# New places for some steps in the hand-set order of every engine, in a fused attention and mixture kernel

## What is computed

```python
x = x + attention(cond(x, side, side, w1, u1, cond_512), Wq, Wk, Wv, Wo, q_scale, k_scale)
x = x + ffn(cond(x, side, side, w2, u2, cond_512), gate_w, mask_up_w, gate_proj_w, up_proj_w, down_proj_w)
```

## Time and profile before

| what | value |
|---|---|
| median of 3 runs | 415.3 us |
| the profiled execution | 415.59 us |
| its span on the core | 413.8 us |
| PE busy | 367.6 us (89%) |
| DVE busy | 326.0 us (79%) |
| ACT busy | 275.6 us (67%) |
| POOL busy | 218.7 us (53%) |
| chain that ended last | PE 66%, DVE 19%, ACT 11%, issue 3% |

### The profile page before, as it was taken

One profiled execution on the slowest core, in us unless ns is written; L12 is line 12 of the kernel. 1 busy time (PEld: TensorE's weight loads), 2 busy tenths in 40 slices (PEclk: granted clock), 3 DMA queues, 4 the chain that ended last, 5 costly groups with the idle time before them and its releaser, 6 DMA issues.

```text
span 413.8 us, 6407 instructions
## 1 busy us (share of the span) xinstructions
PE 367.6 (89%) x1952; PEld 295.0 (71%) x1952; DVE 326.0 (79%) x759; ACT 275.6 (67%) x673; POOL 218.7 (53%) x230
## 2 busy tenths in 40 slices
PE   0098869899999799898999997999899999999996
PEld 0097656688878667687787776687687878788884
DVE  8999789988988997599999889476567777665543
ACT  5547789798789497796978879784274434453321
POOL 7260614278524868134693121563269756888832
PEclk9999999999999999999999999999999999999999
DMA  6825300112100304001031000110065433365121
GB/s 207 308 76 197 104 0 3 49 57 99 52 0 2 103 0 154 1 2 51 2 101 40 1 2 0 38 48 32 2 186 160 140 115 97 96 216 166 53 76 51
DMA packets 14209, 31.92 MB, mean 77 GB/s; under 512 B 1872, under 2 KB 4432, under 8 KB 14176
## 3 DMA queue, kind: packets, MB, share of 16 engines
q1 hardware_dynamic: 13888, 31.38, 23.2%
q10 hardware_dynamic: 288, 0.14, 0.1%
HBM read 30.43 MB, written 1.08 MB: 76 GB/s over the span
## 4 chain that ended last, share of the span: by engine, by line
PE 66%; DVE 19%; ACT 11%; issue 3%; DVEq 0%; ACTq 0%
PE ov L1223 7%; PE sc L1201 7%; PE tr L1152 5%; PE proj L1140 4%; PE acc L1126 3%; PE acc L1128 3%; PE acc L1127 3%; PE proj L1144 3%; PE proj L1141 3%; PE acc L1317 2%; PE acc L1318 2%; PE tr L1127 2%; PE acc L1321 2%; PE tr L1126 2%; PE tr L1128 2%
## 5 line engine op out<-in xcount | busy, mean ns | idle before, releaser
L598 POOL TENSOR_TENSOR WL<-stage,WH 128x256 fp32r<-128x256 f32 x142 | 125.6, 913 | 75.6 <-ACT WH L664 75.6
L612 POOL TENSOR_TENSOR PR<-PR,RI 128x512 f32<-128x512 f32 x48 | 53.7, 1134 | 80.7 <-DVE RI L1072 80.7
L1140 PE MATMUL proj<-WH,RH 128*128 128x512 f32 x96 | 42.5, 442 | 32.0 <-DVE RL L923 19.9
L625 ACT ACTIVATE PR<-PR,MX 128x128 f32<-128x128 f32 (+1 forms) x128 | 56.6, 455 | 0.0
L1201 PEld LDWEIGHTS sc<-kT,QT 128*128 128x128 f32 x256 | 41.0, 191 | 15.8 <-issue 12.8
L1223 PE MATMUL ov<-PTS,V 128*128 128x512 f32 x96 | 46.6, 594 | 1.1 <-DVE OL L1084 1.1
L1201 PE MATMUL sc<-kT,QT 128*128 128x128 f32 (+1 forms) x256 | 47.2, 327 | 0.0
L1140 PEld LDWEIGHTS proj<-WH,RH 128*128 128x128 f32 x96 | 18.4, 192 | 38.6 <-issue 36.3
L1062 DVE CUSTOM_DVE_ANT_0 PR<-sc,const,RQ 128x128 f32<-128x128 f32 (+1 forms) x128 | 45.5, 411 | 0.1
L824 ACT CAST OH<-PR 128x512 fp32r<-128x512 f32 x22 | 13.6, 620 | 41.7 <-DVE PR L1108 41.7
L618 POOL TENSOR_TENSOR OL<-PR,OH 128x512 fp32r<-128x512 f32 x22 | 28.9, 1315 | 22.3 <-ACT OH L824 20.8
(11 more groups left out here) (166 smaller groups left out, 948.4 us busy)
## 6 DMA issues: line engine op xcount, KB each, us to landing
stage<-in_ffn SPq DMA_DIRECT2D x22, 384.0 KB, 3.3
stage<-in_wq SPq DMA_DIRECT2D x8, 512.0 KB, 3.3
stage<-in_wo SPq DMA_DIRECT2D x8, 512.0 KB, 3.3
SBC<-group_scalars SPq DMA_DIRECT2D x8, 256.0 KB, 3.6
PR<-in_tables SPq DMA_DIRECT2D x4, 352.0 KB, 7.4
fT<-in_fT SPq DMA_DIRECT2D x4, 256.0 KB, 4.0
xT<-in_xT SPq DMA_DIRECT2D x4, 256.0 KB, 4.5
stage<-in_wk SPq DMA_DIRECT2D x2, 512.0 KB, 4.9
```

The source lines that it names most:

```text
L598: i = pool.tensor_tensor(lo[:, c:c + 256], src[:, c:c + 256], hi[:, c:c + 256].bitcast(F32), ALU.subtract)
L612: pool.tensor_tensor(pr, pr, RI[:, m % 4, hs[0]:hs[0] + nh].rearrange("p (h o) -> p h o", o=1).broadcast_to([P, nh, 512 // nh]), ALU.mult) ...
L625: return nc.scalar.activation(o, i, ACT.Exp, **k)
L1140: mm(proj[:], rh[ch], wh[ch], start=ch == 0, stop=False, skip_group_check=True)
```

## The change

It moves steps and changes none. At the start, TensorE runs both late table products R6 and R7 ahead of the first query projection; ScalarE casts Q0 behind its copy of K1(0,0); VectorE makes the key weights' low part WL and the next batch's E ahead of RL. In the tiles, VectorE's pattern has "rest" and a "bg" ahead of "D1"; onehot goes from tile 2 to 3; V1's split from 17 to 15; Q7's split from 23 to 25; K3(1,2) and K3(1,3) from 19 to 20; V(1,1) from 21 to 22. All lines below the first insertion carry a number that is one higher in the changed kernel.

```diff
@@ ORDERS
-    "DVE": [("kv", 0), ("kv", 0), ("bg", 0), ("kv", 0), ("bg", 0), ("A", 0), ("D1", 4),
-            ("kv", 0), ("bg", 0), ("F", 6), ("N", 0), ("S", 2), ("rest", 0), ("kv", 0),
+    "DVE": [("kv", 0), ("kv", 0), ("bg", 0), ("kv", 0), ("bg", 0), ("A", 0), ("rest", 0),
+            ("bg", 0), ("D1", 4), ("kv", 0), ("F", 6), ("N", 0), ("S", 2), ("kv", 0),
@@ START
-           ("R", 2), ("R", 3), ("R", 4), ("R", 5), ("K3", 0, 0), ("K3", 0, 1)],
+           ("R", 2), ("R", 3), ("R", 4), ("R", 5), ("K3", 0, 0), ("K3", 0, 1), ("R", 6),
+           ("R", 7)],
@@ START, ACT
-            ("split", "K", 0), ("wkv", 1, 0, 7), ("small",), ("wkv", 1, 1, 1), ("split", "Q", 0), ("K1", 0, 0), ("K1", 0, 1),
+            ("split", "K", 0), ("wkv", 1, 0, 7), ("small",), ("wkv", 1, 1, 1), ("K1", 0, 0), ("split", "Q", 0), ("K1", 0, 1),
@@ START, DVE
-    "DVE": [("wkv", 1, 0, 0), ("wkv", 1, 0, 2), ("wkv", 1, 0, 3), ("wkv", 1, 0, 4), ("wkv", 1, 0, 5), ("wkv", 1, 0, 6), ("wkv", 1, 0, 8),
-            ("wkv", 1, 1, 0), ("split", "K", 0), ("wkv", 1, 1, 2), ("wkv", 1, 1, 3), ("wkv", 1, 1, 4), ("K1", 0, 0), ("K1", 0, 1),
+    "DVE": [("wkv", 1, 0, 0), ("wkv", 1, 0, 2), ("wkv", 1, 0, 3), ("wkv", 1, 0, 4), ("wkv", 1, 0, 5), ("wkv", 1, 0, 6), ("split", "K", 0),
+            ("wkv", 1, 1, 0), ("wkv", 1, 0, 8), ("wkv", 1, 1, 2), ("wkv", 1, 1, 3), ("wkv", 1, 1, 4), ("K1", 0, 0), ("K1", 0, 1),
@@ make_plan
-                  (2, ("onehot",)), (15, ("zeros",)),
-                  (10, ("split", "K", 1)), (17, ("split", "V", 1))):
+                  (3, ("onehot",)), (15, ("zeros",)),
+                  (10, ("split", "K", 1)), (15, ("split", "V", 1))):
...
-    for n, back in enumerate([-2, -2, -2, -1, -3, -2, -2, -3]):
+    for n, back in enumerate([-2, -2, -2, -1, -3, -2, -2, -1]):
...
-    for half, places in (((0, 1), [2, 4, 4, 5, 6]), ((1, 0), [15, 15, 15, 17, 18]), ((1, 1), [17, 18, 18, 19, 19])):
+    for half, places in (((0, 1), [2, 4, 4, 5, 6]), ((1, 0), [15, 15, 15, 17, 18]), ((1, 1), [17, 18, 18, 20, 20])):
...
-    for p, places in ((0, [3, 5, 6, 6]), (1, [21, 21, 23, 24])):
+    for p, places in ((0, [3, 5, 6, 6]), (1, [21, 22, 23, 24])):
```

## The result

The changed kernel takes 416.92 us (median of 5 executions, 416.34 to 417.44), the kernel before 415.3 (5 executions, 415.06 to 415.86). The ratio is 1.0035 with a 95% interval of 1.0024 to 1.0046: 1.0 to 1.9 us slower. The profiled execution of the changed kernel took 417.44, the highest of its five, with a span of 415.6, so its trace holds some more than the median difference (1.8 in the spans, 415.6 against 413.8).

The account below looks back on a forecast made before the run. Chain on VectorE until 42.6 us, then mostly TensorE, waiting for ScalarE's copies. Terms 0.3 + 0.2 + 0.6 + 0.2 = 1.3, given as 1.2 above the 415.3 median: 416.5 us, range 413.6 to 417.8.

Parts of the forecast that it names:

- Edit 1: Start, reordered on TensorE, ScalarE and VectorE: 0.3 us slower, bounds -0.9 and +0.5.
- A(0) comes out at -0.9 or -0.4 + 1.2: Start: VectorE's kept saving of 0.4 to 0.9, plus R7's 1.2, puts A(0) 0.3 to 0.8 us later.
- Edit 2: Onehot moved from tile 2 to 3, ahead of the sum for A(3): 0.2 us slower, bounds 0 and 0.7.
- its first part: Onehot at its new place: 0.41 us on VectorE up to its second instruction.
- Edit 3: V1's split at tile 15, O3's cast behind E(10), delaying K1(1,2)'s copy: 0.6 us slower, bounds 0 and 0.97.
- Edit 4: K3(1,2), K3(1,3), V(1,1) and Q7's split moved later: 0.2 us slower, bounds -1.4 and +0.8.
- Rival A: Start and tiles 19 on: relief of the VectorE-GpSimd lock reaches TensorE, 1.9 us less, 413.4; chance 0.26.
- B: Whole kernel: ScalarE has hidden slack at V1's split, the rest cancels, no difference, 415.3; chance 0.22.
- C: RL behind GWL, onehot at upper bound, V1's split, A(22)'s 0.8 kept: 2.6 us more, 417.9; chance 0.10.

Follow-up runs that it names:

- the three lists alone: Kernel before with only the start's reorderings on VectorE, ScalarE and TensorE: 416.04 us, ratio 1.0012.
- VectorE's list alone: Kernel before with only VectorE's start reordered, WL and E ahead of RL: 414.69 us, ratio 0.9984.
- ScalarE's list alone: Kernel before with only ScalarE's cast of Q0 behind the copy of K1(0,0): 414.98 us, ratio 0.9992.
- GpSimd held back: Changed kernel with one added wait, so GpSimd's gate piece GWL starts behind RL: 415.78 us, ratio 1.0008 to the kernel before.
- VectorE's list and the last edits: Kernel before with VectorE's new start, K3 to tile 20, V(1,1) to 22, Q7's split to 25, wkv(2,2,1) a tile later: 414.48 us, ratio 0.9976.

## Why the prediction was right, and where it was right by luck

Forecast 416.5, measured 416.9, on the side it was expected.

**Edit 1, +0.3:** the three lists alone give +0.5 (0.1 to 0.9). Its steps, one by one: first matmul 0.8 to 1.3 later, measured 1.46 with 0.24 of DMA, so 1.22, near the end where RL pays for GWL; scans at 1.2, yes; VectorE idle before the sum of K1(0,1), yes, 2.04; TensorE idle between A(0) and B(0), yes, 0.68. R7 was priced at 1.2 at A(0), of which ScalarE makes up 0.2 to 0.3 by A(1): 1.19 and 1.05 at these two copies where R7 was moved alone, so this held but for 0.1. One step was wrong. "A(0) comes out at -0.9 or -0.4 + 1.2" takes VectorE as what sets K3. The trace of the kernel without R7's move agrees (K3 0.72 sooner), but the profiled changed kernel has K3 0.57 later, since there TensorE was the later one. I had let TensorE's own way from the first matmul to K3 out of the sum: it was 1.08 ahead of VectorE before, and a first matmul 1.22 later uses up more than that. This is the step that failed. The expectation for VectorE's list alone had TensorE's wait in it and missed too (+0.5 against -0.7), by leaving out what VectorE gains.

**Edit 2, +0.2:** the two instructions take 0.18 and 0.25 at the new place (0.38 and 0.65 before) and ScalarE's wait grew from 0.32 to 0.36. 0.03 in the trace. The term was mis-sized in its first part: the cast holds VectorE for 0.22 there and not for 0.41; the second instruction holds it for 0.17 and E gives back 0.34, as worked out. Neither onehot's move nor the new place of "rest" and "bg" in VectorE's pattern was run alone.

**Edit 3, +0.6:** 0.44 to 0.47 in the traces, 0.7 (0.4 to 1.1) in the time. The step (a cast of 1.07 in place of an idle 0.32) is what the trace shows; the copy of K1(1,2) makes up 0.44 of it and not 0.32. The wait before A(17) was to be 1.4 and is 0.93, because TensorE already waits 0.20 for ScalarE's copy of QT a little ahead of it.

**Edit 4, +0.2:** A(21) and A(22) came out as worked out: -1.94 against -1.9 forecast, +0.81 against +0.8, each taken from the 1.88 at A(17). The wait at D(21,1) went, as forecast. What was mis-sized is what that gives back: the row at 264.01 shows -0.2 for the edit in all, so 1.0 is taken back behind tile 22, and not 0.6. Alone it measured 0.

**The sum.** The runs alone give 0.5 for the start, 0.7 for edit 3 and 0 for edit 4: 1.2 with onehot's 0.03, the forecast's own size, and the changed kernel 1.5 (1.0 to 1.9). That they add holds within the intervals. That the sum fits is in part luck. In the trace of the changed kernel the start is 1.1 above its term and the other three together some 0.7 below theirs (0.03, 0.44 and -0.2 against 0.2, 0.6 and 0.2), and these errors cancel.

Rival A fell. A part of what it counts on is there without R7: VectorE's list alone gives -0.7, but by the wait of 0.68 that it fills, since RL then pays for GWL in a scan's place. Freeing one scan brought K1(0,2) 0.32 sooner with ScalarE's list alone, and nothing behind VectorE's list. Its condition, ScalarE at V(1,1) before TensorE, is met in the kernel with wkv(2,2,1) later, and that is 0.5 faster. B would have been the result without R7's move. C's 0.8 of A(22) was not kept.

## What to carry to other kernels

Where two engines arrive at one place, write down both arrivals before costing a move: one that delays the early engine is free up to its wait, and what goes beyond the wait is paid for. A filler between a projection and its transposes (R7 here) costs nothing while it covers the wait for the copy; ahead of the projection nearly all of it is paid for (1.03 of 1.2). When one step leaves a tile, look at what stands ahead of its copy on the engine that drains the bank: moving those three activations turned a null result into a gain.

## What the runs showed of the hardware

**The lock falls on whichever two-input instruction stands beside GpSimd's piece.** RL took 1.22 beside the gate piece and 0.68 to 0.69 where that piece was held back; a scan 1.69 against 1.20; a sum of squares 0.68 in either case. The Trainium skill (SBUF — State Buffer, "Who interferes with whom") says that the later one to issue is fully blocked and that a reduction never is, and these traces agree with both.

**TensorE starts slowly, for a time that differs from trace to trace.** With nothing before, its first matmuls of 512 columns follow each other by 0.43 us (1.2 GHz by the columns), later ones by 0.23 (near 2.4 GHz), while the page's granted clock is 1.00 in both stretches. The way from the first matmul to R1 holds the same 20 matmuls in every kernel here (14 of them up to the second projection) and took these times:

| kernel | first matmul | to the second projection | to R1 |
|---|---|---|---|
| before | 19.89 | 4.81 | 6.51 |
| changed | 21.35 | 4.82 | 6.86 |
| changed, R7 back | 21.23 | 4.16 | 5.62 |
| GpSimd held back | 20.58 | 4.17 | 5.62 |
| K3 and V(1,1) moved alone | 19.89 | 4.63 | 6.14 |
| the same, wkv(2,2,1) later | 19.88 | 4.82 | 6.42 |
| R7 moved alone | 19.88 | 4.61 | 6.12 |
| VectorE's list alone | 21.11 | 4.82 | 6.50 |
| VectorE's list and the last edits | 21.10 | 4.40 | 5.90 |

The same work takes up to 1.24 more in one execution than in another. The order is not the reason: the changed kernel and the one with R7 back have the same order on every engine up to K3 and took 6.86 and 5.62, and the kernel before and the two with only tiles 19 and later moved took 6.51, 6.14 and 6.42. In the latter three TensorE's wait at K3 (1.08, 1.47 and 1.19) hides the difference: K1(0,2) stands at 44.67 to 44.70 in all of them. In the changed kernel it lies on the path, and the profiled execution has the longest one. With K3 at 32.89, as in the kernel with R7 back, and 11.9 to 12.1 from there, K1(0,2) would stand at 44.8 to 45.0: 0.1 to 0.3 later than before, which is the forecast's term. The trace has it at 46.08. What sets the length of the slow stretch stays open, and so does some 0.5 of the 1.5 us between the changed kernel and the same with R7 back, of which R7's place explains 1.0 to 1.1.

**A second place differs from trace to trace.** Near 312 us, behind the last product of a feed-forward block and ahead of the gate's, TensorE's weight load stands idle, for a time that the profile puts down to no engine: 0.54 us before, 0.75 in the changed kernel, 1.02 with V1's split alone, 0.18 with VectorE's list alone. No edit moves anything there. So traces of two kernels can differ by some 0.4 us behind that place, either way, for no reason of the edit, and what an edit is worth is read ahead of it or from the medians.
